# An attention factorization machine on one core: at most three row gathers in flight, GpSimd waiting for the third one back

## The chip, the core and the metric

One core of a Trainium2 chip. Its engines run side by side, each through its own queue of instructions, and meet only at semaphores: TensorE (PE in the profile; PEld is its weight load), VectorE (DVE), ScalarE (ACT), GpSimd (POOL) and SyncE (SP). Sixteen DMA engines move data between the memory of the chip and the core's on-chip memory. The metric is the time on the device in microseconds (us), the median of several executions; the kernel before takes 842.64 us.

## The reference

For each of 2048 samples there are 32 field indices. Negative indices wrap, others are clipped to the last of 12,500 rows (so most fields of this input read the same row). What is computed, cut to what matters:

```
V = emb_v[x]                                   # [32, 2048, 64]
iu, ju = np.triu_indices(32, k=1)              # 496 pairs
VV = V[iu] * V[ju]
hid = relu(einsum('pbk,kh->pbh', VV, at_w) + at_b)
score = einsum('pbh,ho->pbo', hid, at_h)
pooled = sum(VV * score, axis=0)
logit = pooled @ p + w0 + sum(w1[x], axis=0)
prob = sigmoid(logit)
```

All of it is in float32.

## The kernel before

**Fills.** The batch is cut into 32 fills (`FILLS`) of 64 samples. For a fill the embeddings of its 64 x 32 indices are gathered into one of two buffers `rows` (fill t uses `rows[t % 2]`), 128 rows of 64 numbers at a time: 16 gathers (`GATHERS`) a fill, each an indirect DMA that GpSimd issues (L296). TensorE transposes the buffer in `turn` (L535 to L545; for fill 0 in two halves, `first_turn`), ScalarE copies the result to `V` (`keep_v`), and a fill's work is 16 rounds (`ROUNDS`): VectorE multiplies pairs into `X` (L439), TensorE multiplies by `at_w` (`hidden`, L580), ScalarE applies bias and ReLU (L520), TensorE forms the scores (L596). The scores of the last steps are formed in the next fill. `grams` (L610) computes the weighted products p . VV for the next fill at the end of each.

**Where a fill's rows are wanted.** The rows of fill t+1 are transposed inside fill t, ahead of round 6, in fills 1 and 2 ahead of round 12 (`TURN_BEFORE`, `LATE_TURN`); for fill 1 behind the last round of fill 0.

**The gathers.** Fills 0 and 1 (`PLAIN_FILLS`) gather 64 numbers a row from the given table `emb_v`. From fill 2 on the source is a joint table of 66 numbers a row: `w1`, the embedding, and `w1` again, of which a gather takes 65, so that the linear term comes along. This table is built at the start: SyncE loads `emb_v` in four pieces into space that later belongs to `H`, VectorE copies them to `joined`, and SyncE stores them (semaphore `table_stored`). Only then can fill 2 be gathered. The w1 values of fills 0 and 1 are fetched by 32 small gathers (L306) at the end of GpSimd's queue.

**What paces GpSimd.** GpSimd executes its queue in order. Before the gathers of fill t (from 3 on) it waits until the buffer was transposed (`rows_turned`), its w1 values were copied (`w1_kept`) and the grams of fill t-2 were computed (`gram_ready`); inside a fill, ahead of every fourth gather, it waits for a round of fill t-2 (`z_ready`, `GROUP_AFTER`). Nothing makes it wait for a gather to land. The landings are counted, 16 for each gather, in `first_rows` (fill 0, two semaphores), `second_rows` (fill 1) and `rows_gathered` (two, by the parity of the fill); `turn` waits for one of these to reach the full count.

TensorE's queue for fills 3 to 30 is a loop over two fills; GpSimd's is written out, one instruction after the other.

Of the kernel before, what the change touches and what calls it, by code (L numbers as in the profile page):

```python
# [33 lines left out]
FILL_M = 4  # L34
# [3 lines left out]
GATHERS = 2 * TILES  # L38
# [24 lines left out]
PLAIN_FILLS = 2  # L63
TAIL = (VOCAB - MAIN) // TAIL_RUN
GROUP_AFTER = (0, 3, 7, 10)


def segments(s):
# [27 lines left out]
def afm_kernel(nc, r_x, emb_v, at_w, at_b, at_h, p, w0, w1, out):  # L96
# [11 lines left out]
    with ctx:  # L108
# [6 lines left out]
        def sem(name):  # L115
            return ctx.enter_context(nc.semaphore(name))
# [78 lines left out]
        first_rows = [sem(f"first_rows{g}") for g in range(2)]  # L195
        first_turned = sem("first_turned")
        first_v = sem("first_v")
        second_rows = sem("second_rows")
        rows_gathered = [sem(f"rows_gathered{i}") for i in range(2)]
        rows_turned = sem("rows_turned")  # L200
        w1_kept = sem("w1_kept")
        v_ready = sem("v_ready")
# [17 lines left out]
        def over_fills(eng, fill):  # L220
# [5 lines left out]
                fill(t, 1, False, False)  # L226
                fill(t + 1, 0, False, False)
            fill(FILLS - 1, (FILLS - 1) % 2, False, True)

        def gathered(t, parity):  # L230

            return 16 * GATHERS // 2 * (t - parity)

        def piece(dram, k):

# [15 lines left out]
        @block.sync  # L251
        def _(sp):

            for q in range(QUARTERS // 2):
                load_idx(sp, q)
            for k in range(PIECES):
                load_piece(sp, k)
            sp.dma_start(tail[:, :, 1:1 + EMB], last_rows(emb_v)).then_inc(tail_loaded, 16)
            sp.wait_ge(w1_joined, 4)
            for k in range(PIECES):  # L260
                sp.wait_ge(rows_joined[k], 1)
                store_piece(sp, k)
            sp.wait_ge(tail_loaded, 16)
            sp.dma_start(last_rows(table), tail[:, :, :]).then_inc(table_stored, 16)
            sp.wait_ge(y_ready, 1)
            sp.dma_start(out.rearrange("(q a m) o -> a q (m o)", q=QUARTERS, a=QUARTERS), y_sb[:, :, :]).then_inc(y_stored, 16)
            sp.wait_ge(y_stored, 16)

        @block.gpsimd
        def _(pool):  # L270
            nc.gpsimd.iota(prow_i[:, :], pattern=[[0, 1]], base=0, channel_multiplier=1)
            nc.gpsimd.iota(step_i[:, :, :, :], pattern=[[1, STEPS], [0, FIELDS // STEPS], [-1, STEPS]], base=0,
                           channel_multiplier=0)
            nc.gpsimd.iota(jrow_i[:, :], pattern=[[1, FIELDS]], base=0, channel_multiplier=0).then_inc(iotas_ready, 1)
            nc.gpsimd.memset(ident[:, :], 0.0).then_inc(ident_cleared, 1)
            pool.wait_ge(ident_cleared, 1)
            nc.gpsimd.affine_select(out=ident[:, :], in_=ident[:, :], compare_op=ALU.not_equal, fill=1.0, base=0,
                                    pattern=[[-1, 128]], channel_multiplier=1).then_inc(ident_ready, 1)

            flat = table.rearrange("v (k o) -> (v k) o", o=1)  # L280

            def gather(t, paced=False):

                joint = t >= PLAIN_FILLS
                source, at_rows = (flat, joint_idx) if joint else (emb_v, idx)
                for g in range(2):
                    for m in range(FILL_M):
                        if paced and g == 0 and m == 0:
                            pool.wait_ge(gram_ready, t - 1)
                        elif paced and m % 2 == 0:  # L290
                            pool.wait_ge(z_ready, ROUNDS * (t - 2) + GROUP_AFTER[2 * g + m // 2])
                        for half in range(2):
                            col = (2 * half + g) * NM + t * FILL_M + m
                            c0, c1 = (0, ROW) if joint else (EMB_AT[half], EMB_AT[half] + EMB)
                            arrived = first_rows[g] if t == 0 else second_rows if t == 1 else rows_gathered[t % 2]
                            pool.indirect_dma_start(out=rows[t % 2][:, g * FILL_M + m, half, c0:c1], out_offset=None,  # L296
                                                    in_=source,
                                                    in_offset=bass.IndirectOffsetOnAxis(ap=at_rows[:, col:col + 1], axis=0)
                                                    ).then_inc(arrived, 16)

            plain_w1 = [(Q, n) for n in range(PLAIN_FILLS * FILL_M) for Q in range(QUARTERS)]

            def gather_w1(Q, n):

                at = bass.IndirectOffsetOnAxis(ap=idx[:, Q * NM + n:Q * NM + n + 1], axis=0)
                pool.indirect_dma_start(out=w1_all[:, Q, n:n + 1], out_offset=None, in_=w1, in_offset=at  # L306
                                        ).then_inc(w1_first, 16)

            pool.wait_ge(idx_ready, 1)
            gather(0)  # L310
            pool.wait_ge(idx_ready, 2)
            gather(1)
            pool.wait_ge(idx_ready, 4)
            pool.wait_ge(table_stored, 16 * (PIECES + 1))
            pool.wait_ge(first_turned, 2)
            gather(2)
            for t in range(3, FILLS):
                pool.wait_ge(rows_turned, t - 2)
                pool.wait_ge(w1_kept, 2 * (t - 1 - PLAIN_FILLS))
                gather(t, paced=True)  # L320
            for Q, n in plain_w1:
                gather_w1(Q, n)
# [211 lines left out]
        def _(pe):  # L534
            def turn(t, parity):  # L535

                if isinstance(t, int) and t == 1:
                    pe.wait_ge(second_rows, 16 * GATHERS)
                else:
                    pe.wait_ge(rows_gathered[parity], gathered(t, parity))  # L540
                embs = rows[parity][:, :, :, :].rearrange("p t h k -> p t (h k)")
                for g in range(2):
                    for m in range(FILL_M):
                        last = nc.tensor.transpose(Z[:, TURN_SLOT, g, 128 * m:128 * m + 128],  # L544
                                                   embs[:, g * FILL_M + m, 1:1 + 2 * EMB], ident[:, :])  # L545
                last.then_inc(rows_turned, 1)
# [154 lines left out]
```

## Time and profile before

| what | value |
|---|---|
| time, median of 3 executions | 842.64 us (840.57 to 845.03) |
| the profiled execution | 840.11 us, span 838.3 us |
| mean granted TensorE clock | 0.986 of full speed |
| TensorE busy | 785.2 us, 94% |
| VectorE busy | 721.5 us, 86% |
| ScalarE busy | 640.2 us, 76% |
| GpSimd busy | 568.4 us, 68% |
| indirect gathers of joint rows | 480, mean 1043 ns on GpSimd |
| moved over the span | 24.27 MB, mean 29 GB/s |

The span runs from the first to the last instruction of the profiled execution. What GpSimd is busy with in a gather is the making of it; the data move later, on the DMA engines, and land later still. "Idle before" in a row is the time in which the engine did nothing ahead of that instruction, with what released it; "issue" stands where it waited for nothing that the trace shows.

### The profile page before, as it was taken

What the parts mean: (1) busy time and instruction counts of PE and PEld (TensorE: products, weight loads), DVE (VectorE), ACT (ScalarE), POOL (GpSimd) and SP (SyncE); (2) the same over time, 40 slices, a digit from 0 to 9 for tenths busy, and PEclk for the clock granted to TensorE, in tenths of its full rate; (3) what the DMA queues carried; (4) which work ended last, traced back from release to release, by engine and by line L of the source; (5) the groups of instructions that cost most, each with busy time, mean ns of one, the idle gap of its engine ahead of it and who ended that gap; (6) DMA issues with size and microseconds to landing.
All of it is one profiled execution on the core that took longest, in us unless ns stands there. A gap on an engine that the chain in (4) does not pass through costs nothing.

```text
span 838.3 us, 26331 instructions
## 1 busy us (share of the span) xinstructions
PE 785.2 (94%) x10550; PEld 278.0 (33%) x10550; DVE 721.5 (86%) x1221; ACT 640.2 (76%) x672; POOL 568.4 (68%) x553
## 2 busy tenths in 40 slices
PE   0448999999999999999999999999999999999998
PEld 0113333333333333333333333333333333333332
DVE  2473989899999999999999999999999999999884
ACT  0245778788887878888888788898888888888775
POOL 6727767666677666667676666676766667767772
PEclk9878999999999999999999999999999999999999
DMA  9975859635423446543243448823443435833300
GB/s 182 149 47 22 26 23 25 24 23 22 24 21 23 22 21 22 22 22 24 20 24 22 22 21 22 23 22 22 23 23 21 22 21 23 24 21 23 12 1 1
DMA packets 19910, 24.27 MB, mean 29 GB/s; under 512 B 10472, under 2 KB 10541, under 8 KB 19885
## 3 DMA queue, kind: packets, MB, share of 16 engines
q0 software_dynamic: 17408, 17.07, 47.1%
q1 hardware_dynamic: 1535, 6.64, 2.1%
q10 hardware_dynamic: 942, 0.22, 0.1%
q8 instruction: 16, 0.26, 0.1%
q14 instruction: 9, 0.07, 0.0%
HBM read 20.59 MB, written 3.31 MB: 29 GB/s over the span
## 4 chain that ended last, share of the span: by engine, by line
PE 91%; issue 2%; POOL 2%; DMA 2%; ACT 2%; DVE 1%; ACTq 0%
PE Z L580 55%; PE SG L596 27%; PE SG L610 5%; PE Z L544 4%; POOL rows L296 2%; DMA rows<-in_L_rec_emb_v_dram,idx 2%; ACT H L520 1%; ACT pV L465 1%; DVE X L439 0%; DMA idx_raw<-in_r_x_dram 0%; PE Z L674 0%; PE SG L556 0%; ACT V L454 0%; PE Z L653 0%; ACT y_sb L530 0%
## 5 line engine op out<-in xcount | busy, mean ns | idle before, releaser
L439 DVE TENSOR_TENSOR X<-V 128x992 f32<-128x992 f32 (+15 forms) x1024 | 634.8, 691 | 32.5 <-ACT V L454 18.4
L296 POOL DMA_INDIRECT rows<-table,joint_idx x480 | 500.6, 1043 | 232.5 <-issue 153.8
L520 ACT ACTIVATE H<-Z,bias 128x1024 f32<-128x1024 f32 x512 | 529.3, 1119 | 122.8 <-PE Z L580 119.3
L580 PE MATMUL Z<-X,w_sb 64*64 64x512 f32 x4096 | 479.8, 602 | 14.7 <-issue 10.0
L580 PEld LDWEIGHTS Z<-X,w_sb 64*64 64x64 f32 x4096 | 148.2, 132 | 296.3 <-issue 289.3
L596 PE MATMUL SG<-H,score_w 128*32 128x512 f32 x2048 | 239.5, 597 | 0.0
L596 PEld LDWEIGHTS SG<-H,score_w 128*32 128x32 f32 x2048 | 56.8, 109 | 173.7 <-issue 96.1
L465 ACT ACTIVATE pV<-V,pmask 128x1024 f32<-128x1024 f32 x64 | 81.4, 1276 | 0.1
L407 DVE TENSOR_TENSOR prod<-SG,gram 128x512 f32<-128x512 f32 x32 | 22.1, 691 | 61.8 <-PE SG L596 61.8
L454 ACT COPY V<-Z 128x1024 f32<-128x1024 f32 x31 | 31.4, 1012 | 34.7 <-PE Z L544 34.7
L610 PEld LDWEIGHTS SG<-V,pV 128*32 128x32 f32 x4096 | 42.5, 109 | 23.5 <-issue 18.8
L610 PE MATMUL SG<-V,pV 128*32 128x32 f32 x4096 | 43.1, 198 | 2.0 <-ACT pV L465 1.7
L296 POOL DMA_INDIRECT rows<-in_L_rec_emb_v_dram,idx x32 | 34.8, 1088 | 11.6 <-issue 9.1
L306 POOL DMA_INDIRECT w_all<-in_L_rec_w_dram,idx x32 | 31.6, 986 | 9.8 <-issue 9.8
L544 PEld LDWEIGHTS Z<-ident,rows 128*128 128x128 f32 x248 | 26.5, 140 | 26.7 <-issue 22.6
L544 PE MATMUL Z<-ident,rows 128*128 128x128 f32 x248 | 33.9, 280 | 0.7 <-ACT H L520 0.7
L556 PE MATMUL SG<-ident,rows 128*128 128x128 f32 x8 | 2.2, 431 | 33.1 <-DMA rows<-in_L_rec_emb_v_dram,idx 33.1
L413 DVE TENSOR_REDUCE part<-prod 128x512 f32 (+1 forms) x32 | 21.6, 676 | 0.0
L396 DVE TENSOR_TENSOR gram<-SG,upper_first 128x512 f32<-128x512 f32 x32 | 21.6, 674 | 0.0
L494 ACT COPY V<-SG 128x512 f32<-128x512 f32 x2 | 1.2, 585 | 23.3 <-PE SG L556 23.3
L400 DVE TENSOR_TENSOR gram<-gram,gram_last 128x256 f32<-128x256 f32 x32 | 13.6, 425 | 1.1
L394 DVE TENSOR_TENSOR gram_last<-SG,lower_last 128x256 f32<-128x256 f32 x32 | 13.1, 410 | 1.5 <-PE SG L610 1.5
(46 smaller groups left out, 34.5 us busy)
## 6 DMA issues: line engine op xcount, KB each, us to landing
rows<-table,joint_idx POOLq DMA_INDIRECT x480
table<-joined SPq DMA_DIRECT2D x4, 792.0 KB
H<-in_L_rec_emb_v_dram SPq DMA_DIRECT2D x4, 768.0 KB, 8.6
rows<-in_L_rec_emb_v_dram,idx POOLq DMA_INDIRECT x32, 9.0
w_all<-in_L_rec_w_dram,idx POOLq DMA_INDIRECT x32
idx_raw<-in_r_x_dram SPq DMA_DIRECT2D x2, 64.0 KB, 2.0
idx_raw<-in_r_x_dram ACTq DMA_DIRECT2D x2, 64.0 KB, 2.2
table<-tail SPq DMA_DIRECT2D x1, 54.7 KB
```

Source lines behind the costliest of these rows:

```text
L296: pool.indirect_dma_start(out=rows[t % 2][:, g * FILL_M + m, half, c0:c1], out_offset=None, in_=source, in_offset=bass.IndirectOffsetOnAxi ...
L306: pool.indirect_dma_start(out=w1_all[:, Q, n:n + 1], out_offset=None, in_=w1, in_offset=at).then_inc(w1_first, 16)
L396: nc.vector.tensor_tensor(gram[parity][:, :, :], SG[parity][:, :, :], upper_first[:, :].unsqueeze(1).to_broadcast([128, GROUP, FIELDS]), A ...
L407: nc.vector.tensor_tensor(prod[:, :, :], SG[parity][:, :, :], gram[parity][:, :, :], ALU.mult).then_inc(prod_ready, 1)
L439: last_one = nc.vector.tensor_tensor(xo, vj, vi.unsqueeze(3).to_broadcast(shape), ALU.mult)
L454: nc.scalar.copy(V[parity][:, :, :], Z[:, TURN_SLOT, :, :].rearrange("p g (b f) -> p (g b) f", f=FIELDS)).then_inc(v_ready, 1)
L465: nc.scalar.activation(pV[:, :, half, :, :], V[parity][:, :, :].rearrange("p b (i c) -> p b c i", c=2), ACT.Copy, scale=pmask[:, half:half ...
L520: nc.scalar.activation(H[:, s % H_SLOTS, :, COLS * g:COLS * g + COLS], Z[:, z_slot(t, r), :, :], ACT.Relu, bias=bias[:, 0:1]).then_inc(hid ...
L544: last = nc.tensor.transpose(Z[:, TURN_SLOT, g, 128 * m:128 * m + 128], embs[:, g * FILL_M + m, 1:1 + 2 * EMB], ident[:, :])
L580: done = nc.tensor.matmul(Z[64 * par:64 * par + 64, z_slot(t, r), half, :], w_sb[k, :], X[k, s % X_SLOTS, par, COLS * g:COLS * g + COLS], ...
L596: last = nc.tensor.matmul(SG[parity][at:at + 32, :, :], score_w[:, s, :], hid.rearrange("p (b j) -> p b j", j=FIELDS), start=(s == 0), sto ...
L610: last = nc.tensor.matmul(SG[parity][at:at + 32, b, :], pV[:, g * GROUP + b, half, :, :].rearrange("p c i -> p (c i)"), V[parity][:, g * G ...
```

## The change

Every gather from fill 1 on gets a number n, counted on over the fills. Ahead of gather n, GpSimd waits until gather n - 3 has landed. Landings are counted in four semaphores `rows_landed` that the gathers take in turn (n modulo 4), so that the one waited for is never shared with another gather in flight. `turn` waits for all four, and a no-op keeps these waits apart from the transposes. The gathers of fill 0 and the 32 of w1 are left as they are; so are all other waits, the order of the work and what is computed.

```diff
+LANES, IN_FLIGHT = 4, 3
...
-        second_rows = sem("second_rows")
-        rows_gathered = [sem(f"rows_gathered{i}") for i in range(2)]
+        rows_landed = [sem(f"rows_landed{lane}") for lane in range(LANES)]
...
                         for half in range(2):
+                            n = GATHERS * (t - 1) + 2 * (FILL_M * g + m) + half
+                            if n >= IN_FLIGHT:
+                                pool.wait_ge(rows_landed[(n - IN_FLIGHT) % LANES], 16 * ((n - IN_FLIGHT) // LANES + 1))
...
-                            arrived = first_rows[g] if t == 0 else second_rows if t == 1 else rows_gathered[t % 2]
+                            arrived = first_rows[g] if t == 0 else rows_landed[n % LANES]
...
             def turn(t, parity):
 
-                if isinstance(t, int) and t == 1:
-                    pe.wait_ge(second_rows, 16 * GATHERS)
-                else:
-                    pe.wait_ge(rows_gathered[parity], gathered(t, parity))
+                for lane in range(LANES):
+                    pe.wait_ge(rows_landed[lane], 16 * GATHERS // LANES * t)
+                pe.nop(nofuse=True)
```

GpSimd's queue at the gathers of fill 3 (`rows1` is the buffer of odd fills). Before:

```order
L296 DMA rows1<-table,joint_idx 128x65 [waits gram_ready,w1_kept,rows_turned]
L296 DMA rows1<-table,joint_idx 128x65 x3
L296 DMA rows1<-table,joint_idx 128x65 [waits z_ready]
L296 DMA rows1<-table,joint_idx 128x65 x3
L296 DMA rows1<-table,joint_idx 128x65 [waits z_ready]
```

The same place after the change:

```order
L295 DMA rows1<-table,joint_idx 128x65 [waits gram_ready,rows_landed1,w1_kept,rows_turned]
L295 DMA rows1<-table,joint_idx 128x65 [waits rows_landed2]
L295 DMA rows1<-table,joint_idx 128x65 [waits rows_landed3]
L295 DMA rows1<-table,joint_idx 128x65 [waits rows_landed0]
L295 DMA rows1<-table,joint_idx 128x65 [waits rows_landed1,z_ready]
L295 DMA rows1<-table,joint_idx 128x65 [waits rows_landed2]
L295 DMA rows1<-table,joint_idx 128x65 [waits rows_landed3]
L295 DMA rows1<-table,joint_idx 128x65 [waits rows_landed0]
```

No instruction changed its place; each gather now has a wait of its own, and the first and every fourth has it beside those it had.

TensorE's queue around the transposes of an odd fill inside the loop (`Z` is the result bank, `ident` the unit matrix). Before:

```order
L596 MATMUL SG1<-H,score_w 32x512 x3
L544 MATMUL Z<-ident,rows1 128x128 [waits rows_gathered1,hid_ready]
L544 MATMUL Z<-ident,rows1 128x128 x7
L569 REGISTER_ALU
L580 MATMUL Z<-X,w_sb 64x512 [waits x_ready,hid_ready]
```

After:

```order
L594 MATMUL SG1<-H,score_w 32x512 x3
L537 ISA [waits hid_ready]
L542 MATMUL Z<-ident,rows1 128x128 [waits rows_landed3,rows_landed2,rows_landed0,rows_landed1]
L542 MATMUL Z<-ident,rows1 128x128 x7
L567 REGISTER_ALU
L578 MATMUL Z<-X,w_sb 64x512 [waits x_ready,hid_ready]
```

The transposes stand where they stood and wait for four counts instead of one.

## Rows read from the trace of the kernel before

**Rows 1.** The page: busy time of each engine, DMA share in 40 slices, chain by engine

```profile
PE 785.2 (94%) x10550; PEld 278.0 (33%) x10550; DVE 721.5 (86%) x1221; ACT 640.2 (76%) x672; POOL 568.4 (68%) x553
...
DMA  9975859635423446543243448823443435833300
...
PE 91%; issue 2%; POOL 2%; DMA 2%; ACT 2%; DVE 1%; ACTq 0%
```

**Rows 2.** Timeline of TensorE, 446 to 471: start us, us, engine line op xcount

```profile
446.82 5.54 PE L580 MATMUL Z<-X,w_sb 64*64 64x512 f32 x48
...
454.15 1.09 PE L544 MATMUL Z<-ident,rows 128*128 128x128 f32 x8
...
470.91 4.59 PE L580 MATMUL Z<-X,w_sb 64*64 64x512 f32 x40
```

**Rows 3.** Timeline of GpSimd, 443 to 472; in brackets the idle time before

```profile
443.67 0.94 POOL L296 DMA_INDIRECT rows<-table,joint_idx  x1 [0.30 <-issue]
447.57 1.86 POOL L296 DMA_INDIRECT rows<-table,joint_idx  x1 [2.96 <-PE SG L610]
...
471.65 1.60 POOL L296 DMA_INDIRECT rows<-table,joint_idx  x1 [2.91 <-PE SG L610]
```

**Rows 4.** Timeline of TensorE, fill 0 to fill 4

```profile
62.62 5.39 PE L580 MATMUL Z<-X,w_sb 64*64 64x512 f32 x21 [8.32 <-issue]
...
75.04 1.10 PE L544 MATMUL Z<-ident,rows 128*128 128x128 f32 x8 [0.67 <-ACT H L520]
...
140.16 1.09 PE L544 MATMUL Z<-ident,rows 128*128 128x128 f32 x8
```

**Rows 5.** Timeline of VectorE, products of fill 0

```profile
50.62 9.71 DVE L439 TENSOR_TENSOR X<-V 128x736 f32<-128x736 f32 x16
```

**Rows 6.** One window: busy time by engine, then PEclk, DMA share, GB/s

```profile
60.30:60.40 0.10, 0.00 (x0) 0.00 (x0) 0.03 (x1) 0.00 (x0) 0.00 (x0) 0.50 0.59 164
```

**Rows 7.** The page's DMA queues: packets, MB, share of 16 engines

```profile
q8 instruction: 16, 0.26, 0.1%
```

**Rows 8.** The chain of waits: start us, us, what

```profile
26.49 14.48 DMA rows<-in_L_rec_emb_v_dram,idx
```

**Rows 9.** Timeline of GpSimd, fills 1 and 2

```profile
28.08 1.03 POOL L296 DMA_INDIRECT rows<-in_L_rec_emb_v_dram,idx  x1 [0.30 <-issue]
...
47.67 0.95 POOL L296 DMA_INDIRECT rows<-in_L_rec_emb_v_dram,idx  x1 [0.30 <-issue]
64.58 0.94 POOL L296 DMA_INDIRECT rows<-table,joint_idx  x1 [15.96 <-issue]
```

**Rows 10.** Windows after a burst's last gather, and at the first table gather

```profile
446.80:446.90 0.10, 0.07 (x4) 0.10 (x8) 0.10 (x1) 0.00 (x0) 0.00 (x0) 1.00 0.92 42
446.90:447.00 0.10, 0.10 (x4) 0.10 (x8) 0.10 (x1) 0.00 (x0) 0.00 (x0) 1.00 0.00 0
66.20:67.40 1.20, 1.20 (x8) 0.13 (x2) 0.00 (x0) 1.05 (x1) 0.90 (x2) 0.50 0.33 28
```

**Rows 11.** Timeline of all engines at the first gather

```profile
3.90 0.17 DVE L337 TENSOR_SCALAR idx<-prod 128x16 uint32<-128x16 f32 x1
...
4.36 1.12 POOL L296 DMA_INDIRECT rows<-in_L_rec_emb_v_dram,idx  x1 [2.14 <-DVE idx L337]
```

**Rows 12.** Windows over 16 gathers in two fills

```profile
133.70:154.70 21.00, 21.00 (x188) 6.51 (x184) 20.39 (x34) 18.72 (x20) 16.42 (x16) 1.00 0.95 25
157.60:180.00 22.40, 22.38 (x192) 7.47 (x189) 19.59 (x33) 19.12 (x21) 17.51 (x16) 1.00 0.36 24
```

**Rows 13.** Timeline of TensorE and GpSimd at the end

```profile
791.85 1.09 PE L544 MATMUL Z<-ident,rows 128*128 128x128 f32 x8
...
822.12 0.94 POOL L306 DMA_INDIRECT w_all<-in_L_rec_w_dram,idx  x1 [0.30 <-issue]
...
832.54 1.05 PE L653 MATMUL Z<-w_all,pick 32*4 32x128 f32 x32
```

More of the change, by code:

```diff
@@ L228, in over_fills @@
             fill(FILLS - 1, (FILLS - 1) % 2, False, True)
-        def gathered(t, parity):
-            return 16 * GATHERS // 2 * (t - parity)
         def piece(dram, k):
```

## The prediction, made before the changed kernel was run

> **What bounds the kernel now.** I read the page's busy shares and the chain that ended last first. TensorE is busy for 94% of the span and makes 91% of the chain; the rest is the first 85 us [rows 1]. Then the timeline of TensorE in the steady part: fill after fill it works without a gap, and a fill's first matmuls follow those of the fill before by 470.91 - 446.82 = 24.09 us [rows 2]. So in the steady part nothing that GpSimd does is paid, as long as the rows of the next fill are there when the transposes want them. The transposes of one fill start at 454.15 [rows 2], so those of the next at 454.15 + 24.09 = 478.24; the gathers for these start at 447.57 [rows 3], 30.7 us ahead. GpSimd spends 0.94 + 0.30 = 1.25 us on a plain repetition (0.30 idle "issue") [rows 3], and after the last of 16, started at 443.67, it waits for the grams until 447.57 [rows 3]. Its budget for a gather is 24.09 / 16 = 1.505 us; above that, GpSimd is the bound of the whole kernel.
>
> The start is different. TensorE stands still for 8.32 us before 62.62, and the trace names no engine or transfer for it, only "issue" [rows 4]. VectorE meanwhile goes on and has all products of fill 0 ready at 50.62 + 9.71 = 60.33 [rows 5]. Just before TensorE resumes, at 60.30, one window of 0.1 us moves 164 GB/s x 0.1 us = 16.4 KB [rows 6]; the queue of instructions has 16 packets of 0.26 MB, also 16 KB each [rows 7]. I read this as TensorE out of instructions, with their transfer late behind the gathers: the last gather of fill 0 took 14.48 us from issue to landing in that stretch [rows 8], and 16 more were issued from 28.08 to 47.67 without waiting [rows 9].
>
> **The change, part by part.**
>
> *The limit in the steady part.* A gather now starts at the later of 1.25 us after the last start and the landing of the third one back plus the time GpSimd takes to react. Three gathers per (latency + reaction). For the latency, from start of the instruction: the last gather of a burst starts at 443.67 [rows 3] and its last data move before 446.90, nothing after it [rows 10], 3.2 us. The first table gather, alone in flight, starts at 64.58 [rows 9] and its data are through by about 67.4 [rows 10], 2.8 us. The semaphore write behind the data has no row; between 0 and 0.79 us (the slowest reaction below); I take 0.5 and so 3.7 us. For the reaction: with a single wait, VectorE's index ends at 3.90 + 0.17 = 4.07 and GpSimd starts at 4.36, 0.29 us [rows 11]. With several waits in front, the grams end at 446.78 (the next matmuls start at 446.82 [rows 2]) and GpSimd starts at 447.57, about 0.79 us [rows 3]. After the change 12 of the 16 gathers of a fill have one wait and 4 have more, so (12 x 0.29 + 4 x 0.79) / 16 = 0.42 us. The pitch is (3.7 + 0.42) / 3 = 1.37 us. Landings are uneven, and an early one earns nothing below 1.25 us while a late one is paid, so I add 0.1 us (an estimate): 1.47 us, against 1.505 that are free. Bounds: 1.25 us (3 x 1.25 = 3.75 is more than 2.8 + 0.29, so with quick landings the limit never acts) and (3.2 + 0.79 + 0.79) / 3 = 1.59 us.
>
> The Trainium skill ("DMA: Bandwidth & Descriptors", section "Anatomy of one DMA — SWDGE (gpsimd) path") puts a GpSimd DMA at about 2.0 us plus bytes over 436e3, which is 2.1 us for these 33 KB; by it the pitch would stay 1.25 us and the steady part would not notice the limit. The windows show data moving 3.2 us after the start, so I don't use it.
>
> *Slow stretches.* Over the same 16 gathers the DMA engines are busy for 0.36 of one stretch and 0.95 of another [rows 12], with the same bytes. Some 1.2 us of data time [rows 10] then become up to 1.2 x 0.95 / 0.36 = 3.2 us, latency 5.7 us and pitch 2.0; with fewer in flight I take the middle, latency 4.6 and pitch 1.67. The page's DMA slices show such fills five or six times [rows 1]. The mean pitch is (24 x 1.47 + 6 x 1.67) / 30 = 1.51 us: as good as the budget. A single slow fill costs 16 x (1.67 - 1.505) = 2.6 us of GpSimd's lead, and the lead is 478.24 - (471.65 - 3.9 + 3.7) = 6.8 us, so single ones are swallowed ([rows 2, 3]; the last start of a burst lies 447.57 - 443.67 = 3.9 us before the next burst).
>
> *TensorE's waits.* The transposes wait for four semaphores instead of one, and a no-op follows: 31 times three more instructions in TensorE's queue. TensorE shows no gap before the transposes (the row of 454.15 has no idle time in it [rows 2]), its queue runs ahead of the array. Cost 0; if that cover were gone, 31 x 4 x 0.05 = 6 us, the 0.05 an estimate near the 0.04 us that follow a landing in the chain [rows 8].
>
> *The start.* Fill 1's gathers fall under the limit too, fill 0's don't. The first three go at 28.08 and after, as now. The fourth waits for the first of them, which is queued behind fill 0's last, landed at 26.49 + 14.48 = 40.97 [rows 8]: about 42.4. Twelve more pitches follow, five at 1.7 us while the table is still being stored (an estimate between 1.47 and 2.0) and seven at 1.47: the sixteenth at 61.2, landed at 64.9; the first gather of the table at 62.7, against 64.58 now [rows 9]. If the instructions then arrive in a gather's latency, some 4 us instead of more than 8, TensorE follows VectorE, is done with the hidden layers soon after 60.33 [rows 5] and transposes fill 1 at 65.0 when its rows land, where it does at 75.04 now [rows 4]: 10 us earlier. What is late next is GpSimd. Behind each waiting gather all later ones are queued, and at the end the 32 of w1. The last row of fill t lands at 62.7 + (16(t-1) - 1) x pitch + 3.7. For fill 4 with pitch 1.50 (one slow fill among the three) that is 136.9, and its transposes start at 140.16 now [rows 4]: only 3.3 of the 10 us are kept. For fill 31 with 1.51 it is 62.7 + 479 x 1.51 + 3.7 = 789.7 against 791.85 [rows 13]: 2.2 early. The last w1 gather starts at 822.12, lands some 3 us later and is wanted at 832.54 [rows 13]: 7 us to spare, which cover this.
>
> **The sum.** Steady part 0, TensorE's waits 0, start -10 given back to -3. The profiled execution was 840.11 us with a span of 838.3; it would be 837. The median of the runs is 842.64, 2.5 above the profiled one, and the forecast is 842.64 - 3 = **839.6 us**.
>
> **Rivals.**
> *GpSimd becomes the bound.* The point is a mean pitch of 1.515 us, (791.85 - 62.7 - 3.7) / 479. Above it each 0.01 us costs 4.8 us, since TensorE waits at every transposition. At 1.55 us: 62.7 + 742.5 + 3.7 - 791.85 = +17, so 860 us; at the upper bound of 1.59 us +36, so 879. For it: my own mean is 1.51, the slow stretches, and the slowest of 16 DMA engines decides each landing. Against it: fewer gathers in flight should shorten each.
> *The start gains nothing.* The stall isn't the gathers' doing. Then everything stays as now and the limit hides in the 6.8 us lead: 842.6. For it: the trace names no cause. Against it: the idle time ends just when the queue of gathers has drained.
> The Trainium skill (same page, section "Queues, rings and completion order") says that a DMA engine takes turns between the queues it has work for; by that rule the instructions' transfer would wait for one packet and not for the backlog, and this rival would be the truth.
> *The start keeps most of its gain.* Pitch 1.40 in the first fills: fill 4 lands at 62.7 + 47 x 1.40 + 3.7 = 132.2, 8 us early: 834.6.
>
> **How the numbers follow.** The measurement of this kernel can tell about 0.5%, 4.2 us, from no change. Forecast (gain of 0 to 5 us) 0.40, of which 0.15 lies beyond 838.4; start gains nothing 0.15; gain kept 0.10; GpSimd bound 0.35, nearly all above 846.9. Faster 0.25, same 0.40, slower 0.35. The range leaves out 0.05 below and 0.15 above: 833 to 868. The likeliest case alone would be 837 to 843.
>
> **What would show it.** The starts of GpSimd's gathers: a pitch of 1.45 to 1.50 us in an ordinary fill, and a gap before the next fill's first gather; if that gap is gone in every fill and TensorE waits for "DMA rows" at the transposes, GpSimd is the bound. The "issue" gap of TensorE in fill 0 below 2 us, transposes of fill 1 near 65, those of fill 4 near 137. The forecast is wrong if the pitch is over 1.515 on average, or if the 8.32 us stay.

## The result, and the profile after

The changed kernel takes 895.03 us (median of four runs, 885.6 to 909.93) beside 841.84 us for the kernel before. Two of the four runs (899.61 and 909.93 us) lie over 1.5% above the fastest and are left out of the ratio, which is 1.0543 with an interval of 1.0471 to 1.0614. It is slower by 5%, where the forecast was 839.6 us and the range ended at 868. The profiled execution took 890.45 us.

The page of the changed kernel: the span, the busy shares, the chain by engine, the group of GpSimd's table gathers and that of the transposes (busy, mean ns of one | idle time before, and what ended it).

```profile
span 888.6 us, 26496 instructions
PE 802.2 (90%) x10550; PEld 287.7 (32%) x10550; DVE 721.3 (81%) x1221; ACT 640.9 (72%) x672; POOL 636.0 (72%) x553
PE 76%; POOL 12%; DMA 6%; issue 4%; ACT 1%; ACTq 0%; DVE 0%; POOLq 0%
L295 POOL DMA_INDIRECT rows<-table,joint_idx x480 | 566.0, 1179 | 206.6 <-issue 115.0
L542 PE MATMUL Z<-ident,rows 128*128 128x128 f32 x248 | 38.5, 305 | 43.1 <-DMA rows<-table,joint_idx 43.1
```

TensorE was 94% busy and 91% of the chain before [rows 1]. Now 12% of the chain is GpSimd's and 6% the gathers' data, and the transposes, which waited only once before (0.67 us [rows 4]), wait 43.1 us for rows. GpSimd's busy time has grown from 568.4 [rows 1] to 636.0 us with the same instructions, by 67.6 us. That is the first lead: a longer wait between gathers would be idle time, not busy time. Some gathers themselves last longer.

TensorE's timeline says when the loss comes.

```profile
53.16 3.50 PE L578 MATMUL Z<-X,w_sb 64*64 64x512 f32 x24 [0.16 <-DVE X L438]
64.79 1.06 PE L542 MATMUL Z<-ident,rows 128*128 128x128 f32 x8 [1.83 <-DMA rows<-table,joint_idx]
...
141.36 1.94 PE L542 MATMUL Z<-ident,rows 128*128 128x128 f32 x8 [7.14 <-DMA rows<-table,joint_idx]
...
422.33 1.09 PE L542 MATMUL Z<-ident,rows 128*128 128x128 f32 x8
...
453.77 1.94 PE L542 MATMUL Z<-ident,rows 128*128 128x128 f32 x8 [7.28 <-DMA rows<-table,joint_idx]
...
480.29 1.09 PE L542 MATMUL Z<-ident,rows 128*128 128x128 f32 x8
...
842.24 1.09 PE L542 MATMUL Z<-ident,rows 128*128 128x128 f32 x8
```

The 8.32 us for nothing are gone: TensorE follows VectorE at 53.16. Fill 1 is transposed at 64.79, 10.2 us earlier than 75.04 [rows 4]. By fill 4, with a wait of 7.14 us before its transposes, that is used up (141.36 against 140.16 [rows 4]), and by fill 31 the kernel is 842.24 - 791.85 [rows 13] = 50.4 us late. From fill 4 on most of the loss comes in four jumps (fills 7, 16, 24 and 28), each a wait of 7 to 9 us before the transposes, and one stands in the rows: from 422.33 to 480.29 two fills take 57.96 us instead of 2 x 24.09 = 48.18 [rows 2]. Apart from fill 5 (27.25 us), the jumps and the fill behind each, a fill takes 24.1 to 24.9 us.

GpSimd's timeline ahead of that jump, with the start's and the last table gather:

```profile
42.10 1.76 POOL L295 DMA_INDIRECT rows<-in_L_rec_emb_v_dram,idx  x1 [10.70 <-DMA rows<-in_L_rec_emb_v_dram,idx]
...
62.43 0.95 POOL L295 DMA_INDIRECT rows<-table,joint_idx  x1 [0.55 <-issue]
...
425.48 0.94 POOL L295 DMA_INDIRECT rows<-table,joint_idx  x1 [0.30 <-DMA rows<-table,joint_idx]
427.34 14.13 POOL L295 DMA_INDIRECT rows<-table,joint_idx  x1 [0.92 <-PE Z L578]
441.78 1.09 POOL L295 DMA_INDIRECT rows<-table,joint_idx  x1 [0.30 <-issue]
...
833.57 0.95 POOL L295 DMA_INDIRECT rows<-table,joint_idx  x1 [0.30 <-issue]
```

One gather lasts 14.13 us where its neighbours take 0.94 to 1.1. In the whole trace there are four of this kind (13.75 us at 198.10, 14.13 at 427.34, 14.19 at 631.92, 13.78 at 738.97), all the ninth of their fill, and one of 4.24 us at 85.61; no other table gather reaches 2 us. The window in the middle of the long one has GpSimd busy throughout and not a byte moving (columns: busy time of PE, PEld, DVE, ACT, POOL, then PEclk, DMA share, GB/s):

```profile
429.00:441.00 12.00, 11.96 (x228) 4.63 (x224) 12.00 (x22) 9.03 (x11) 12.00 (x1) 1.00 0.00 0
```

So no data are late there: the instruction sits on GpSimd without producing its transfer. VectorE is busy for all 12 us beside it (TensorE for 11.96; the experiments tell the two apart). VectorE's timeline:

```profile
425.48 0.68 DVE L412 TENSOR_REDUCE part<-prod 128x512 f32 x1
426.07 14.58 DVE L438 TENSOR_TENSOR X<-V 128x608 f32<-128x608 f32 x24
440.56 0.43 DVE L393 TENSOR_TENSOR gram_last<-SG,lower_last 128x256 f32<-128x256 f32 x1
```

24 products run back to back, each starting some 80 ns before the last ends (their mean duration is 690 ns, their distance 14.58 / 24 = 608). The last ends at 440.65, the held gather at 427.34 + 14.13 = 441.47, 0.82 us behind. An ordinary gather takes 0.94 us: this one seems to run its first 0.1 us, stand until the products are through, and then do the rest. The clock adds to it. The window behind TensorE's wait has a granted clock of 0.72, where it was 1.00 [rows 12]:

```profile
453.00:461.00 8.00, 7.23 (x49) 3.19 (x49) 3.31 (x5) 4.24 (x5) 5.87 (x7) 0.72 0.29 22
```

In finer windows the granted clock is 0.50 (1.2 GHz) from 453 to 457 us, behind 7.28 us of idling, and 1.00 (2.4 GHz) from 458 on; the eight transposes take 1.94 us instead of 1.09. So a jump costs more than its wait.

### The profile page after: what moved, and what is told of

Same layout as the page of the kernel before. It is cut to its first block, busy times and chain, and to the rows that moved or that the text cites. A ratio compares the mean times of both kernels' runs of the same rounds, so it can differ in the third digit from the quotient of the medians.

```text
span 888.6 us, 26496 instructions
## 1 busy us (share of the span) xinstructions
PE 802.2 (90%) x10550; PEld 287.7 (32%) x10550; DVE 721.3 (81%) x1221; ACT 640.9 (72%) x672; POOL 636.0 (72%) x553
## 4 chain that ended last, share of the span: by engine, by line
PE 76%; POOL 12%; DMA 6%; issue 4%; ACT 1%; ACTq 0%; DVE 0%; POOLq 0%
PE Z L578 46%; PE SG L594 21%; POOL rows L295 12%; PE SG L608 5%; PE Z L542 4%; DMA rows<-table,joint_idx 3%; DMA rows<-in_L_rec_emb_v_dram,idx 3%; ACT pV L464 1%; ACT H L519 1%; DMA idx_raw<-in_r_x_dram 0%; PE Z L672 0%; ACT V L453 0%; PE Z L651 0%; ACT y_sb L529 0%; ACT w_all L471 0%
## 5 line engine op out<-in xcount | busy, mean ns | idle before, releaser
L295 POOL DMA_INDIRECT rows<-table,joint_idx x480 | 566.0, 1179 | 206.6 <-issue 115.0
L542 PE MATMUL Z<-ident,rows 128*128 128x128 f32 x248 | 38.5, 305 | 43.1 <-DMA rows<-table,joint_idx 43.1
L608 PEld LDWEIGHTS SG<-V,pV 128*32 128x32 f32 x4096 | 47.6, 109 | 28.7 <-issue 22.6
L608 PE MATMUL SG<-V,pV 128*32 128x32 f32 x4096 | 51.8, 199 | 3.4 <-ACT pV L464 1.6
L542 PEld LDWEIGHTS Z<-ident,rows 128*128 128x128 f32 x248 | 30.4, 155 | 69.4 <-issue 69.4
```

The source lines that it names most:

```text
L608: last = nc.tensor.matmul(SG[parity][at:at + 32, b, :], pV[:, g * GROUP + b, half, :, :].rearrange("p c i -> p (c i)"), V[parity][:, g * G ...
```

## Why only some gathers are held

The kernel before has the same run of products, and its gathers go through it without a long hold (0.94 to 1.40 us). VectorE and GpSimd, kernel before:

```profile
433.23 0.67 DVE L413 TENSOR_REDUCE part<-prod 128x512 f32 x1
433.82 14.78 DVE L439 TENSOR_TENSOR X<-V 128x608 f32<-128x608 f32 x24
```
```profile
434.47 0.95 POOL L296 DMA_INDIRECT rows<-table,joint_idx  x1 [0.30 <-issue]
435.73 0.94 POOL L296 DMA_INDIRECT rows<-table,joint_idx  x1 [0.30 <-issue]
```

What differs is the moment. The sum over pairs (TENSOR_REDUCE) ends at 433.90; the gathers start 0.57 and 1.83 us behind it. In the changed kernel the held one starts 427.34 - 426.16 = 1.18 us behind it. Its row puts this start down to TensorE, which is not so: the round that it waits for had ended at 424.49, and the gather three back landed at 426.60, 0.74 us before the start. It is the new wait that sets the moment, here and in front of the other three long ones, each 0.74 us behind a landing. I measured the distance from the sum for every gather from fill 3 on, in the traces of before, after and 17 of the experiments:

| | starts 0.60 to 1.79 us behind the sum, VectorE going on for 0.8 us or more | of these held over 2 us |
|---|---|---|
| before | 0 | 0 |
| after | 14 | 5 |
| four in flight, with breaks, same kind of chip | 0 | 0 |
| all 19 traces | 76 | 38 |

GpSimd's unhindered beat of 1.25 us steps over this stretch in every fill (0.10 or 0.57 us, then 1.83). A gather that has waited for a landing comes at any moment: in the changed kernel 14 in 29 fills fall into the stretch, and a third of these are held, in all traces half. The stretch was drawn after the fact, around where the long holds start, and why a start in it is dangerous, and only half the time, is not known. It does not hold all of them either: 25 of the 63 holds over 2 us lie outside, 22 of them 2 to 6.1 us long at the first gather of a fill, but also one of 8.22 us that starts 7.14 us behind the sum (`e2`) and one of 13.44 us at 1.88 (`i2`). The end is more regular. All 63 gathers held over 2 us from fill 3 on end 0.81 to 0.83 us after the end of a product, and in 62 of them this is a product behind which VectorE pauses or turns to another operation.

## The experiments

Two kinds of chips were given for them, and only ratios inside one group of runs are comparable. On four chips the kernel before takes 1122 to 1160 us, since TensorE there has breaks for which the trace names no cause. On the last chip it takes 836.53 us, like the chip of the prediction (842).

**The limit in fill 1 alone, from fill 2 on alone, and with four in flight.** `e1`, `f2`: as before but, in fill 1, four lanes and

```
+ if IN_FLIGHT <= n < GATHERS:
+     pool.wait_ge(rows_landed[(n - IN_FLIGHT) % LANES], ...)
```

`e2`, `f3`: `if n >= GATHERS + IN_FLIGHT`, fill 1 as before. `e3`, `f4`: the change with `LANES, IN_FLIGHT = 4, 4`.

> The limit is kept for the 16 gathers of fill 1 alone; from fill 2 on everything is as in the kernel before. Theory A (the start gains, and the loss comes from the limit in the later fills): TensorE's transposes of fill 1 again near 65 us instead of 75, no gather instruction over 5 us on GpSimd after 60 us, and the time is 10 us below the kernel before, about 832. Rival (the gain of the start is taken back wherever GpSimd's first table gather at 62 us sets the pace): 838 to 842.

> The limit is kept from the fourth gather of fill 2 on, and fills 0 and 1 are gathered as in the kernel before. Theory A (single gather instructions are held for about 14 us by VectorE's unbroken run of products, and TensorE then waits for rows): two to six such instructions, start as before (transposes of fill 1 at 75 us), time 885 to 915, as the changed kernel plus up to 10. Rival (the loss comes from fills 1 to 5, where the pitch was slow): 842 to 850.

> Four gathers in flight instead of three. At a pitch of 1.25 us four back is 5.0 us, more than the usual landing. Theory A: GpSimd is seldom stopped, so seldom starts a gather out of its rhythm; none or one instruction of 14 us, start still gains, 830 to 842. Rival B (a limited number in flight by itself brings the long instructions): as many as with three, 880 or more.

> The limit in fill 1 alone. Theory A: transposes of fill 1 near 65 us, no hold over 5 us in the later fills, 828 to 833, 10 to 12 us below the kernel before. Rival (what the start gains is taken back at GpSimd): 838 to 842.

> The limit from fill 2 on, none in fill 1. Theory A: start as in the kernel before, two to six holds of 8 to 14 us, TensorE waits for rows, 870 to 910. Rival (the loss needs the early start): 842 to 850.

> Four in flight. Theory A (a gather is held when it starts out of rhythm after a wait; four back is 5.0 us and seldom stops GpSimd): 0 to 2 holds, 830 to 850. Rival (any limit does the same): 880 or more, four or more holds.

Measured on chips with the kernel before at 1131.27 and 1159.56 us: fill 1 alone 1.0033 [0.996, 1.0106] and 1.0079 [1.004, 1.0118]; later fills alone 0.972 [0.9656, 0.9785] and 0.9755 [0.9662, 0.9848]; four 1.0197 [1.013, 1.0264] and 1.0139 [1.0072, 1.0206]. None came out as expected, and for the limit from fill 2 on and for four the sign was the other way round. I put this down to TensorE's breaks, which rule on these chips; these runs don't show it. The start did not gain here either: fill 1 was transposed at 98.67 us in `e1` and 97.06 in `f2`, later than in `e2` (80.20) and `f3` (76.89), which have no limit in fill 1. With the limit the first 16 KB packet of the queue of instructions came at 50.0 and 49.7 us instead of 61.4 and 59.8, as on the chip of the prediction (48.8 instead of 60.3), but TensorE then worked through fill 0 in short pieces with "issue" breaks between them. So the gain of the start is shown for one kind of chip only. The traces nevertheless showed the same holds: 8.90, 8.22 and 13.59 us in `e2`, 8.80 in `f3`, 9.73 in `e3`, 9.58 in `f4`, and in `e1` and `f2` none over 2 us after fill 5 (6.06 and 6.03 us in fill 3).

**The limit with breaks in VectorE's run.** `e4`, `f1`, `g2`, `h2`: the change, and in VectorE's products

```
+ if not first and r in (0, 2, 4, 6, 14):
+     dve.wait_ge(x_ready, ROUNDS * t + r)
```

VectorE waits for its own product of the round before, which opens a gap of some 35 ns (104 ns once) behind the products that ended a hold.

> The changed kernel, and VectorE waits for its own last product ahead of rounds 0, 2, 4, 6 and 14 of every fill but the first, which puts a break of some 0.03 us in its run of products at most 2.5 us apart. Theory A (GpSimd's instruction is held as long as VectorE's operations follow each other without a break, and let go at the first one): no gather instruction over 4 us from fill 2 on, TensorE no longer waits for rows for 7 us and more, time 830 to 838. Rival B (the 14 us are GpSimd's own or the DMA queue's, say a ring that has to be cleared): they stay, 885 to 910.

> The changed kernel with VectorE's breaks ahead of rounds 0, 2, 4, 6 and 14, on another chip if there is one: on the last one the kernel before took 1131 us, with TensorE idle for 'issue' all along. Theory A (gather instructions are held by VectorE's unbroken run and let go at its first break): none over 4 us after 60 us (on the slow chip the longest was 2.5), TensorE hardly waits for rows, 828 to 838 beside 842 of the kernel before. Rival B (the holds are GpSimd's or the DMA queue's own): several of 13 to 14 us, 880 or more.

> The changed kernel once more, as it is, to have it beside the next run on one chip. Theory (VectorE's unbroken run of products holds single gather instructions of GpSimd for up to 14 us, and each hold delays a fill's transposes): three to five gathers of over 13 us from fill 2 on, ratio to the kernel before 1.04 to 1.07 where that one takes about 842 us. Rival (the holds were a matter of that one execution): none over 5 us, ratio 0.995 to 1.005. On a chip where the kernel before takes 1130 us or more, VectorE breaks more often for itself, and the holds are shorter than 10 us: ratio 0.97 to 1.00.

> The changed kernel with five more waits in each fill: at rounds 0, 2, 4, 6 and 14 VectorE waits for its own product of the round before, which breaks its run for some ten ns. Theory: no gather over 3 us from fill 2 on, the start's gain stays, the transposes wait under 2 us in nearly all fills; 828 to 838 us where the kernel before takes 842 (ratio 0.984 to 0.996). Rival (GpSimd is held by something else, a full queue or its instruction fetch): holds of 13 to 14 us stay, ratio as that of the changed kernel itself, 1.04 to 1.07. Where the kernel before takes 1130 us or more: the ratio at or under that of the changed kernel beside it, 0.965 to 0.975.

`e4` gave 0.9681 [0.961, 0.9751], `f1` 0.965 [0.9575, 0.9725]. With the unmodified change on the same chip (before: 1126.52 us): `g1` 0.9938 [0.9884, 0.9992], `g2` 0.9784 [0.9684, 0.9884]. The ratios of `g1` and `g2` lie in and just above what was expected for such a chip (0.97 to 1.00, 0.965 to 0.975). The change alone held gathers for 13.60 and 9.75 us; in the four traces with breaks none from fill 2 on lasts over 2.51 us, though 12 gathers started in the bad stretch and 10 of these passed 2 us. They end 0.81 or 0.82 us after the product in front of the first gap. This is what the theory wanted and the rival (a full queue, instruction fetch) did not.

**The breaks without the limit.** `h1`: the kernel before with the same added lines; `h2` beside it the limit with breaks.

> The kernel before with the five waits in each fill by which VectorE's run of products is broken (rounds 0, 2, 4, 6 and 14), and no limit on the gathers. Theory (the waits help only by ending holds of GpSimd, and the kernel before has hardly any: 2.84 us once from fill 2 on): ratio 0.997 to 1.004, both where the kernel before takes 842 us and where it takes 1130. Rival (breaking VectorE's run is worth something by itself, whatever the gathers do): the 0.016 by which the limit with the breaks stood under the limit alone shows here too, ratio 0.98 to 0.99.

> The limit of three with the five breaks, on the chip of the run beside it. Theory: no gather over 3 us from fill 2 on; 828 to 838 us where the kernel before takes 842; where it takes 1130, a ratio of 0.965 to 0.98, under the breaks alone. Rival (the holds come from elsewhere): holds of 13 to 14 us and a ratio of 1.04 to 1.07 where the kernel before takes 842; the same ratio as the breaks alone where it takes 1130.

`h1` 1.0096 [1.0041, 1.015], `h2` 0.9777 [0.9692, 0.9861]. The breaks alone cost 1% on this chip, more than the 0.4% I allowed. With the limit they gained 1.5% (`g2` beside `g1`, whose intervals touch), which fits holds being ended but is no proof of it.

**With fewer scoring matmuls.** I wanted TensorE faster, to have VectorE's run as unbroken as on the chip of the prediction. In `i1` (before), `i2` (limit) and `i3` (limit and breaks) 18 of 32 scoring matmuls of a fill are left out:

```
+ if 0 < s < STEPS - 1 and 2 * g + half < 3:
+     continue
```

> The kernel before with 18 of the 32 scoring matmuls of each fill left out (so the scores are not the reference's), to have TensorE faster, about 28 us a fill where the chips of these runs give 33 to 34: VectorE then breaks less, as in the profiled run of 840 us. It is the base for the next two; no forecast of theories hangs on it but that it holds no gather over 3 us from fill 6 on.

> The changed kernel with the same matmuls left out. Theory (the limit puts gathers where VectorE's run of products has no break, and a faster TensorE leaves it fewer breaks): three or more gathers of over 8 us from fill 6 on, more than the limit has with all its matmuls, and 1 to 6% over the base beside it. Rival (the loss of the changed kernel has to do with the chip that it was timed on, and the holds are of no account here): at or under the base, 0.97 to 1.00 of it, as with all matmuls.

> The limit and the five breaks in VectorE's run, with the same matmuls left out. Theory: no gather over 3 us, and the time of the limit alone falls by what its holds cost, to 0.95 to 0.99 of the base. Rival: as the limit alone.

Against the kernel before at 1121.96 us: 1.0018 [0.9956, 1.0079], 0.972 [0.9628, 0.9811], 0.9582 [0.9481, 0.9682]. As a means it failed. The scoring group of `i1`, then of the unmodified change on a chip of the same kind:

```profile
L598 PE MATMUL SG<-H,score_w 128*32 128x512 f32 x896 | 248.4, 613 | 0.0
```
```profile
L594 PE MATMUL SG<-H,score_w 128*32 128x512 f32 x2048 | 247.8, 615 | 0.0
```

896 records keep TensorE busy as long as 2048 do. Three of four matmuls of a group are gone in most rounds, so the four must have run side by side, in the time of one. And `i2` is under its base, not over it. But the holds are the starkest of all. `i2`, GpSimd and VectorE (its trace is of its longest execution, 1122.89 us, so only its holds are read here, not its time):

```profile
520.72 14.57 POOL L295 DMA_INDIRECT rows<-table,joint_idx  x1 [0.30 <-issue]
```
```profile
519.30 0.68 DVE L412 TENSOR_REDUCE part<-prod 128x512 f32 x1
519.89 14.58 DVE L438 TENSOR_TENSOR X<-V 128x608 f32<-128x608 f32 x24
```

0.74 us behind the sum, 14.57 us long, ended at 535.29, 0.82 us after the run's end at 534.47. `i2` has six holds over 8 us after fill 5, `i1` two of 14.6 us in fills 5 and 6, though it has no limit and none over 3 us was expected from fill 6 on. So a hold does not need the limit; what it needs is the moment. `i3` has none over 2.7 us; its ratio is 1.4% below that of `i2`, with intervals that overlap.

**No gathers at all.** `i4`: the kernel before, the 480 gathers of fills 2 to 31 replaced (their rows are a constant):

```
+ if t >= 2:
+     nc.gpsimd.memset(rows[...][:, ..., half, c0:c1], 0.5).then_inc(arrived, 16)
+     continue
```

> The kernel before with the gathers of fills 2 to 31 replaced by small fills of the same tiles by GpSimd (480 gathers and their data gone; the rows of these fills are a constant). Theory on the breaks of TensorE that these chips show (about 165 us in the profiled run of the changed kernel, 0.127 of the time in which data of gathers is in flight and 0.019 of the other time): they come with the gathers' traffic and go with it, under 40 us from fill 3 on, and the time falls from about 1130 us to under 1000. Rival (they are the chip's own): they stay at 130 to 170 us and the time falls by under 30 us.

872.64 us, 0.7804 [0.7727, 0.7882], where before takes 1121.96, as expected. First the page's span and rows of `i4`, then the product matmuls of the unmodified change on a chip of this kind (`g1`):

```profile
span 870.5 us, 26448 instructions
L583 PE MATMUL Z<-X,w_sb 64*64 64x512 f32 x4096 | 480.7, 604 | 47.8 <-issue 23.8 <-DVE X L442 11.5 <-ACT V L457 11.2
L297 POOL MEMSET rows<- 128x65 f32 x480 | 49.9, 154 | 671.1 <-PE SG L613 342.6 <-PE Z L583 312.0 <-DMA table<-tail 16.2
```
```profile
L578 PE MATMUL Z<-X,w_sb 64*64 64x512 f32 x4096 | 592.2, 632 | 86.6 <-issue 79.1 <-DVE X L438 2.1
```

Two transposes in a row of `i4`:

```profile
450.15 1.09 PE L547 MATMUL Z<-ident,rows 128*128 128x128 f32 x8
...
474.23 0.98 PE L547 MATMUL Z<-ident,rows 128*128 128x128 f32 x7
```

Without the gathers TensorE needs 24.08 us a fill on this chip too. So its breaks there come with the gathers, not with the chip alone. `i4` is still above 837 us because the 32 gathers of w1 are left in it: behind them TensorE stands three times for 11 us in fill 30 (33 us, two of these marked "issue").

```profile
768.88 13.55 POOL L309 DMA_INDIRECT w_all<-in_L_rec_w_dram,idx  x1 [0.35 <-issue]
```
```profile
767.02 14.58 DVE L442 TENSOR_TENSOR X<-V 128x608 f32<-128x608 f32 x24
```

The first of them is held too, 1.77 us behind a sum, and ends at 782.43, 0.83 us after VectorE's run: a gather from another table, in a kernel with no limit. Where the breaks of `g1` stand is less clear. From fill 3 on they fill 16.2% of the time up to 3.7 us after a gather's start and 1.9% of the rest, but by the packets themselves 15.0% of the time with one under way and 10.7% of the rest; the first split also divides a fill into its parts, so it doesn't show a cause. None of this explains why a limit of three gains on these chips and one of four loses.

**Two and four in flight, with breaks.** `j1`, `j2`: the kernel with breaks and `LANES, IN_FLIGHT = 4, 2` and `4, 4`. These came on the chip with the kernel before at 836.53 us.

> At most two gathers in flight, with the five breaks in VectorE's run. Theory on the chips of these runs (TensorE's breaks come with the gathers' traffic, and the fewer gathers stand in a line the shorter a break is): the ratio lies under that of three in flight with the breaks (0.965, 0.978 and 0.978), at 0.93 to 0.97, as long as GpSimd's 16 gathers fit into a fill (16 by 1.7 to 2.0 us, 27 to 32 us, against fills of 33 us); longest gather under 3 us. Rival (the number in flight is of no account): the ratio of three, 0.96 to 0.98. Where the kernel before takes 842 us and a fill 25 to 27, GpSimd becomes the bound: 880 us or more, 1.05 or over.

> At most four in flight, with the breaks. Four without the breaks stood at 1.020 and 1.014, three without at 0.994. Theory (the holds are one share of the difference, the number in flight the other): no gather over 3 us and a ratio of 0.98 to 1.005, over that of three with the breaks. Rival (the four lost by its holds alone): 0.965 to 0.98, as three. Where the kernel before takes 842 us: 826 to 838 us, since GpSimd never waits for four and nothing is held.

`j2` takes 830.36 us, within the 826 to 838 expected, 0.9935 [0.9911, 0.9958]: a small gain on the kernel before, but clear of noise. `j1` takes 1063.84 us, 1.2716 [1.2671, 1.276]. The page and TensorE's timeline of `j2`:

```profile
span 828.5 us, 26564 instructions
PE 784.4 (95%) x10550; PEld 278.1 (34%) x10550; DVE 734.9 (89%) x1221; ACT 640.0 (77%) x672; POOL 569.7 (69%) x553
L545 PE MATMUL Z<-ident,rows 128*128 128x128 f32 x248 | 33.8, 279 | 0.8 <-ACT H L522 0.8
```
```profile
64.53 1.06 PE L545 MATMUL Z<-ident,rows 128*128 128x128 f32 x8 [0.76 <-ACT H L522]
...
129.95 1.09 PE L545 MATMUL Z<-ident,rows 128*128 128x128 f32 x8
...
781.98 1.09 PE L545 MATMUL Z<-ident,rows 128*128 128x128 f32 x8
```

The start's 10 us are there (64.53 against 75.04), whole at fill 4 (129.95 against 140.16 [rows 4]) and at fill 31 (781.98 against 791.85 [rows 13]), and the transposes never wait for rows. The kernel before was profiled on another chip, so the measured gain is the ratio, 0.65% or 5.4 us. Its sum and gathers in the steady part:

```profile
423.32 0.67 DVE L413 TENSOR_REDUCE part<-prod 128x512 f32 x1
```
```profile
424.09 1.43 POOL L296 DMA_INDIRECT rows<-table,joint_idx  x1 [0.30 <-PE Z L581]
425.82 0.95 POOL L296 DMA_INDIRECT rows<-table,joint_idx  x1 [0.30 <-issue]
```

0.10 and 1.83 us behind the sum. With four in flight GpSimd keeps its beat (1.36 us from gather to gather in 22 of 30 fills, 1.35 in most of the kernel before) and never starts in the bad stretch, so here the breaks had nothing to do. `j1` does start in it, 18 times (16 with VectorE going on as in the table), 6 of them held, none over 2.56 us from fill 3 on. Its holds end, on this kind of chip too, at a gap in VectorE's run; the gap is there VectorE's wait for TensorE, 1.8 to 3.4 us long, and not the added break. One of them, GpSimd first:

```profile
859.81 2.56 POOL L296 DMA_INDIRECT rows<-table,joint_idx  x1 [1.64 <-DMA rows<-table,joint_idx]
```
```profile
858.47 0.68 DVE L413 TENSOR_REDUCE part<-prod 128x512 f32 x1
859.07 2.49 DVE L441 TENSOR_TENSOR X<-V 128x608 f32<-128x608 f32 x4
864.92 1.29 DVE L441 TENSOR_TENSOR X<-V 128x544 f32<-128x544 f32 x2 [3.37 <-PE Z L581]
```

The products end at 861.56, the gather at 862.37, 0.81 us later. `j1`'s own loss is another matter, that of the rival "GpSimd becomes the bound": the chain of waits by engine and two transposes in a row,

```profile
PE 43%; DMA 39%; issue 8%; POOL 8%; ACT 0%; POOLq 0%; DVE 0%; ACTq 0%
```
```profile
607.85 1.94 PE L545 MATMUL Z<-ident,rows 128*128 128x128 f32 x8 [5.36 <-DMA rows<-table,joint_idx]
...
639.05 1.94 PE L545 MATMUL Z<-ident,rows 128*128 128x128 f32 x8 [5.59 <-DMA rows<-table,joint_idx]
```

31.2 us for 16 gathers, a pitch of 1.95 us, and each transposition waits. Two share a round of latency and reaction of 3.9 us, where the prediction had 3.7 + 0.42 = 4.12. I had expected 880 us "or more", which is far from the 1063.84 measured: 16 pitches of 1.95 us alone make a fill of 31 us, 7 more than before.

## Why the prediction was wrong

*The start: right.* The table below sets its numbers beside the trace.

| | forecast | after |
|---|---|---|
| fourth gather of fill 1 starts | 42.4 | 42.10 |
| first table gather starts | 62.7 | 62.43 |
| fill 1 transposed | 65.0 | 64.79 |
| TensorE's 8.32 us of "issue" [rows 4] | below 2 | gone |
| fill 4 transposed | 137 | 141.36 |
| mean pitch of table gathers | 1.51 | 1.61 |
| the same without the five held ones | | 1.49 |

The rival "the start gains nothing" fell with it on this kind of chip. The prediction had read the rule of turns between queues that the Trainium skill gives ("DMA: Bandwidth & Descriptors", section "Queues, rings and completion order") as saying that the stall would stay. It went when the gathers were limited, so that reading did not hold here; whether the rule itself is at fault isn't shown. On the other kind of chip the packet came early too and the start still lost (`e1`, `f2`), so a late packet is not the whole account of the stall.

*The pitch: right in its ordinary part.* In the 25 fills without a held gather the distance from gather to gather inside a fill is 1.41 to 1.61 us, 1.46 in the mean, and the next fill's first gather starts 1.3 to 2.9 us behind the last one, where the kernel before has 3.9 in most fills, so there is still slack between the fills. The forecast for an ordinary fill was 1.45 to 1.50. The reaction to a landing was 0.26 us with one wait and 0.74 with two (forecast 0.29 and 0.79), and the gather in front of the long one of fill 16 landed 3.77 us after its start (forecast 3.7). What the prediction called the plain repetition, 1.25 us, is not the pitch of the kernel before: that is 1.35 us in most fills. From 62.43 to 833.57 there are 479 distances, 1.610 us each. The five held gathers took 4.24 + 13.75 + 14.13 + 14.19 + 13.78 = 60.1 us, 55.4 more than five ordinary ones; without that the mean is 1.49 us, under the 1.51 of the forecast and the budget of 1.505.

*The step that failed: "A gather now starts at the later of ..."*, the model of the limit in the steady part. It prices when a gather starts and takes the 0.94 us that it lasts as given. A landing wait also moves the start against VectorE's run, and there a gather can last 14 us. The term was missing from the sum, from the bounds of the pitch and from the rivals. Its size: each hold of 14 us adds 13 us to GpSimd's queue where single slow fills were to be swallowed by a lead of 6.8 us; the next transposes wait 7 to 9 us, and with the slower clock behind the wait the two fills cost 9.8 us in the jump shown and 41.6 us in all four. From fill 4 to fill 31 the loss is 50.4 - 1.2 = 49.2 us; of the other 7.6 us, 2.2 lie in fill 5, behind the wait of fill 4, and the rest in fills that are 0.2 to 0.8 us longer than before, for which the trace names no wait. I read the same sign before the run and passed over it: gathers of 1.86 and 1.60 us in [rows 3] are the same hold at its smallest, at the tail of VectorE's run (447.57 + 1.86 = 449.43).

*Fill 4* came 4.4 us later than forecast, and the gather of 4.24 us in fill 3, 3.3 us longer than ordinary, is most of that.

*"GpSimd becomes the bound"* had the right sign and 0.35, but not the mechanism: outside the held gathers the changed kernel's pitch stays in its budget. `j1` shows that rival as it was meant.

*The range* ended at the upper cases of the pitch that I could see. A hold has a chance in each fill and a price of 10 to 12 us, so the number of holds could scatter the runs; only one execution was traced, so this isn't shown for 885.6 to 909.93.

What stays open. Three in flight with breaks was not run on a chip of the 840 us kind, nor four without breaks. That holds make most of the 50 us is read from the trace of the changed kernel, and that the added breaks end them is shown by four traces on the other chips (`e4`, `g2`, `h2`, `i3`); on a chip of this kind `j1` shows only that a longer gap does, and no run took the holds alone out of the changed kernel there. Why a start in the bad stretch is held in one fill and not in the next is open as well. Why TensorE is slowed by the gathers' traffic on some chips and not on others is not known.

## What to carry to other kernels

A limit in flight is a wait, and a wait moves the start of every instruction behind it; look at what the neighbours of that engine do at the new moments, not only at how long it waits. Where GpSimd issues gathers beside a VectorE that runs without a gap, one instruction of a usual 0.94 us may last until VectorE's run ends, so leave the beat alone where it is safe, or put a short break into the run. Choose the smallest limit that in the steady state hardly ever acts: on chips of the 840 us kind four (with breaks) kept the gain of the start, three turned 10 us gained into 50 lost, two (with breaks) made GpSimd the bound. And look at more than one chip: on the others three gained and four lost.

## What the runs showed of the hardware

GpSimd's gather can be held by VectorE's TENSOR_TENSOR with both inputs in SBUF. The run that held the gather at 427.34 was 24 such products, and the hold ended with the products, though VectorE went straight on with an operation that takes one input from PSUM (`gram_last<-SG,lower_last`, started at 440.56, before the last product's end). The Trainium skill ("SBUF — State Buffer", section "Who interferes with whom") says that a VectorE instruction with two SBUF inputs contends with a GpSimd instruction that reads SBUF and not with one that only writes it, and that the loser blocks fully. The trace agrees: the gather reads its indices from SBUF, and the fills in `i4`, which only write, took 154 ns in the mean. The same section also says, as an inference, that `tensor_tensor` does not stall a DMA of GpSimd, since making its descriptors needs the write side; here it did, for up to 14.7 us, and the measurement decides. The section speaks of the whole instruction; here the hold went over 24 instructions. That the read of the indices is what is held wasn't tested apart.

The same chip type gives TensorE quite different times under gather traffic: 1126 and 836.5 us for one kernel, with the limit of three at 0.994 on a chip of the slower kind and 1.054 on one of the faster. Without the gathers of fills 2 to 31 `i4` took 872.6 us on a chip of the slower kind. A change that only moves traffic is worth measuring on both.
